# A four-network GNN kernel on one Trainium2 core: the third mask row loaded ahead of the bias, the second attention unit summed ahead of the third turn, and the count diagonal read behind the next rows

## What is computed

```python
def _gat_layer(x, src, dst, W, a_src, a_dst, bias, concat):
    h = (x @ W).reshape(N, H, C)
    al_s = jnp.einsum('nhc,hc->nh', h, a_src)
    al_d = jnp.einsum('nhc,hc->nh', h, a_dst)
    e = jax.nn.leaky_relu(al_s[src] + al_d[dst], NEG_SLOPE)
    m = jax.ops.segment_max(e, dst, num_segments=N)
    ex = jnp.exp(e - m[dst])
    denom = jax.ops.segment_sum(ex, dst, num_segments=N)
    alpha = ex / (denom[dst] + 1e-16)
    out = jax.ops.segment_sum(h[src] * alpha[:, :, None], dst, num_segments=N)
    ...
    return out + bias
loops = jnp.arange(N, dtype=edge_index.dtype)
src = jnp.concatenate([edge_index[0], loops])
dst = jnp.concatenate([edge_index[1], loops])
h = jax.nn.elu(_gat_layer(x, src, dst, W1, att_src1, att_dst1, b1, concat=True))
out = _gat_layer(h, src, dst, W2, att_src2, att_dst2, b2, concat=False)
```

## Time and profile before

| | |
|---|---|
| median of 3 runs | 3439.72 us (3429.32 to 3456.67) |
| profiled execution, its own time | 3440.88 us |
| its span in the trace | 3439.1 us |
| PE, DVE, ACT, POOL busy | 3217.4, 2175.2, 1337.0, 931.8 us |
| mean granted clock of PE | 0.961 |

### The profile page before, as it was taken

The page is one execution under the profiler, slowest core; times in us unless marked ns, Lnnn a source line. Parts: engine busy times, 40 slices in busy tenths (PEclk is TensorE's granted clock), DMA queues, the critical chain, the costliest instruction groups (busy, mean ns, idle before and its releaser), DMA issues. The chain is left out here.

```text
span 3439.1 us, 61776 instructions
## 1 busy us (share of the span) xinstructions
PE 3217.4 (94%) x20813; PEld 3007.6 (87%) x20813; DVE 2175.2 (63%) x4034; ACT 1337.0 (39%) x2527; POOL 931.8 (27%) x968
## 2 busy tenths in 40 slices
PE   6888999999998999999998999999999897899997
PEld 6876777888887999999997899999988586899997
DVE  7888546667686631018877610228878565499998
ACT  1344233333323121115546411124446330488885
POOL 1102633544545330005447400014447200000000
PEclk9988999999999999999999999999999889899998
DMA  3133344223222353347777643348767400300001
GB/s 81 46 90 121 113 128 106 64 66 108 59 50 69 90 153 100 102 131 236 238 215 234 178 132 103 103 152 244 242 193 237 140 30 15 74 1 0 0 0 46
DMA packets 164966, 386.06 MB, mean 112 GB/s; under 512 B 34418, under 2 KB 103583, under 8 KB 164758
## 3 DMA queue, kind: packets, MB, share of 16 engines
q0 software_dynamic: 47200, 173.39, 16.9%
q1 hardware_dynamic: 80074, 147.20, 15.2%
q10 hardware_dynamic: 37484, 62.75, 6.0%
HBM read 283.93 MB, written 99.32 MB: 111 GB/s over the span
## 5 line engine op out<-in xcount | busy, mean ns | idle before, releaser
L1872 PE MATMUL bank<-w_hi,xT_hi 128*125 128x384 f32 x1920 | 650.6, 339 | 0.0
L1873 PE MATMUL bank<-w_lo,xT_hi 128*125 128x384 f32 x1920 | 648.9, 338 | 0.0
L1874 PE MATMUL bank<-w_hi,xT_lo 128*125 128x384 f32 x1920 | 648.9, 338 | 0.0
L1560 ACT COPY arena<-bank 125x384 f32<-125x384 f32 x320 | 153.8, 480 | 793.8 <-PE bank L1874 765.3
L830 POOL DMA_INDIRECT arena<-y_early,edges x204 | 229.7, 1126 | 817.7 <-DMA y_late<-arena 320.0
L904 DVE SCALAR_TENSOR_TENSOR row_lo<-arena,edges,row_hi 128x768 fp32r<-128x768 f32 x300 | 304.1, 1014 | 125.5 <-ACT row_hi L873 84.1
L2339 DVE CAST w_hi<-w_raw 128x2304 fp32r<-128x2304 f32 x35 | 47.6, 1359 | 517.3 <-PE bank L1874 511.0
L743 ACT ACTIVATE arena<-arena,low 125x1250 f32<-125x1250 f32 x170 | 227.7, 1339 | 334.1 <-DVE low L755 334.1
L1872 PEld LDWEIGHTS bank<-w_hi,xT_hi 128*125 128x125 f32 x1920 | 356.8, 186 | 0.0
L1873 PEld LDWEIGHTS bank<-w_lo,xT_hi 128*125 128x125 f32 x1920 | 356.6, 186 | 0.1
L1874 PEld LDWEIGHTS bank<-w_hi,xT_lo 128*125 128x125 f32 x1920 | 356.6, 186 | 0.1
(11 more groups left out here) (359 smaller groups left out, 6636.6 us busy)
## 6 DMA issues: line engine op xcount, KB each, us to landing
y_early<-arena SPq DMA_DIRECT2D x200, 180.0 KB
w_raw<-in_L_gnn_W_dram ACTq DMA_DIRECT2D x30, 1152.0 KB, 6.3
arena<-own_mask_d SPq DMA_DIRECT2D x50, 585.9 KB
y_late<-arena SPq DMA_DIRECT2D x120, 180.0 KB
h_d<-arena ACTq DMA_DIRECT2D x40, 250.0 KB
arena<-in_L_gnn_W_dram SPq DMA_DIRECT2D x5, 1536.0 KB, 10.5
arena<-h_d ACTq DMA_DIRECT2D x30, 250.0 KB
wadj_d<-arena SPq DMA_DIRECT2D x10, 625.0 KB
```

The lines of the kernel that those rows point to most:

```text
L1872: pe.matmul(b, xT_hi[:, k, v], w_hi[:, h, k], start=(k == 0), stop=False)
L1873: pe.matmul(b, xT_hi[:, k, v], w_lo[:, h, k], start=False, stop=False)
L1874: ins = pe.matmul(b, xT_lo[:, k, v], w_hi[:, h, k], start=False, stop=(k == KD - 1))
```

## The change

Four edits. SP issues the load of mask row 2 ahead of the wait for `al_done` and the bias load. PE sums unit 1 ahead of turning unit 2 and the hidden row of unit 0; ACT runs the exponential of unit 2 behind the high parts of unit 1 instead of ahead of them. DVE reads the count diagonal behind the hot rows of window 4d + 3 instead of ahead of them. No instruction is added or removed.

```diff
--- before.py
+++ after.py
@@ -1096,11 +1096,12 @@
                     load_mask(0)
             sp.wait_ge(h_made, unit(H0 * NT - 1))
             load_mask(1)
-            sp.wait_ge(al_done, H0 * NT)
-            load_b1(0)
             for u in range(2, H0 * NT):
                 h, d = divmod(u, NT)
                 load_mask(u)
+                if u == 2:
+                    sp.wait_ge(al_done, H0 * NT)
+                    load_b1(0)
                 if h and d == 2:
                     sp.wait_ge(hidden_ready, unit(h * NT - 1))
                     load_b1(h)
@@ -1482,9 +1483,11 @@
                         act_hidden_high(act, u - 2)
                     if more:
                         load_next(h + 1, s)
+                    if u == 1:
+                        act_unit_exp(act, u + 1, u + 1, score[:, (u + 1) % 2])
                     if s == 1:
                         act_elu(act, u - 1)
-                    if s + 2 < NT:
+                    if s + 2 < NT and u:
                         act_unit_exp(act, u + 2, u + 2, score[:, u % 2])
                     if more and s == 2:
                         act_row_turn(act, h + 1, bank[2][0:NT, 256:256 + P])
@@ -1811,6 +1814,8 @@
                     u = h * NT + s
                     if more and s == 3:
                         pe.wait_ge(al_ready, h + 2)
+                    if u == 2:
+                        pe_sum(pe, u - 1, [3 + (u - 1) % 2], lambda t: [h_hi[t]], lambda t: [h_lo[h % 2][t]])
                     if s < NT and (s or not h) and u != 1:
                         pe_unit_turn(pe, u, score[:, s % 2])
                     if s >= 2:
@@ -1818,7 +1823,7 @@
                     if more and s == NT:
                         pe.wait_ge(turned_taken, piece(u - 1, 2))
                         pe_s_row(pe, h + 1, 0)
-                    if 1 <= s <= NT:
+                    if 1 <= s <= NT and u != 2:
                         pe.wait_ge(hidden_ready, unit(u - 3))
                         if u == 1:
                             pe.wait_ge(s_row_ready, 1)
@@ -2133,7 +2138,6 @@
                 if d >= 1 and i == 3:
                     if d >= 3:
                         finish_own(d - 3)
-                    count_own(d - 1)
                 if d >= 2 and i == 1:
                     take_log(d - 2)
                 at = d * P + WIN * i
@@ -2146,6 +2150,8 @@
                                                  feat[:, bass.ds(t, 1), R:FC].rearrange("p o c -> p (o c)").unsqueeze(2).to_broadcast([128, 4, WIN]),
                                                  op0=ALU.is_equal, op1=ALU.mult)
                         dve.tensor_scalar(hot_src[:, k], iota_half, edge[:, SRC, bass.ds(t, 1)], None, op0=ALU.is_equal).then_inc(hot_ready[k], 1)
+                if d >= 1 and i == 3:
+                    count_own(d - 1)
                 if w:
                     weight_sum(w - 1)
             weight_sum(NW - 1)
```

## The result

| | before | after |
|---|---|---|
| median of 20 runs | 3437.89 us (3426.75 to 3458.37) | 3419.02 us (3408.87 to 3448.40) |
| ratio of after to before | | 0.9944, 95% interval 0.9924 to 0.9965 |
| profiled execution, span | 3440.88 us, 3439.1 us | 3441.28 us, 3439.5 us |

The change makes the kernel 18.9 us faster; 3421 had been forecast. But the profiled execution of the changed kernel is among the slowest four of its twenty, and as long as that of before. So a comparison of the two spans would say "no change", and the traces have to be compared stage by stage.

What follows compares the result with a forecast made beforehand. PE sets the pace in projection and attention; DVE and PE wait for each other in counting. Counting 14 + attention 6.6 - clock 2 = 18.6, say 19 us: 3440 - 19 = 3421, range 3404 to 3437 (8 in 10).

Steps and rivals of the forecast that it cites:

- rival 2: Counting gets its clock back: 14 + 9 = 23 us there and attention 6.6, giving 3410; chance 0.12.
- Counting, idle time: Counting, read behind hot rows: PE's late hot rows mostly vanish, 14 us won (low end 8, high end 17.7).
- what ACT takes back: Third block of counting: ACT's count copy, straight behind the logarithms, takes back about 0.6 of PE's 1.3 us.
- Counting, clock: Counting: behind one wait PE ran at 1.2 GHz, 0.54 us more a tile, 2.2 a window; not in the sum.
- Recurring waits: By the skill's rule on waits recurring at each step, counting wins more than 14 us and attention only 2.3.
- Mask row 2: Start of attention: load issued near 498.2 instead of 508.48, landing near 506.5, in time for DVE at 511.45.
- The new order: First attention units, played through with old durations: hidden turn of unit 1 at 535.1 against 541.71, gain 6.6 us.
- The uncovered wait: Ahead of L612, the logit row's turn: PE stands 4.4 us for DVE's low parts of unit 2.
- The clock behind that wait: Product part 0 in attention may run at the lower clock, up to 4.3 us more; 2 charged.
- Slower: Counting: PE stands a little in every window and drops to half clock more often, 3452; chance 0.04.
- waits that only move: Counting: DVE's waits only move from L2100 to its ring slots, 3435; chance 0.03.

Runs made afterwards that it cites:

- the second group: Runs on another chip, with the changed kernel unedited against the kernel before: medians 3418.65 against 3452.67 us, ratio 0.9910 (0.9875 to 0.9944).
- the second pair: Second profiled executions of the unedited kernel before and the unedited changed kernel: projection starts at 310.8 and 294.6 us.
- three waits: Kernel before with DVE's wait for ACT's copy also at the heads of the second and third windows: 3511.84 us, ratio 1.0214.
- order only: Kernel before with only the new order on PE and ACT, mask row 2 still loaded late: ratio 1.0008 (0.9972 to 1.0044).
- logits last: Changed kernel with the last network's four-column logit products behind all wide feature products: median 5.6 us above the changed kernel's.
- before again: Kernel before, unedited, profiled a second time: median 4.2 us above the kernel before in the same group, projection at 310.8 us.

## Why the prediction was right, point by point

- **The total.** 3421 forecast, 3419.0 measured, range 3404 to 3437. The ratio says 12 to 26 us faster; the second group puts the change at 34, the interval there 19 to 43. A sum of 19 was at the low side of what all groups together show. That 3421 was met within 2 us is partly luck: the stages of the traces add up to 23 or 24 us (16.2 or 17.3 in counting, 6.9 in attention), inside both intervals but not 19, and rival 2, with 0.12, describes counting better than the forecast does.
- **Counting, idle time.** 14 us had been taken from PE's sum in the earlier trace rows; PE's waits for hot rows fell by 12.2, to 4.3 where about 2 had been expected, and the nine waits of DVE are gone. But other waits, for ACT's count copies above all, came in their place, and PE's idle time fell by 8.4 us only (9.0 in the second pair). The term was too high by 5 to 6 us: of what ACT takes back 0.6 had been seen, in one block, and not charged. The read ended where it was expected to: ACT waits in the first two blocks alone, 0.56 and 1.85 us, where up to 1.6 had been expected once or twice.
- **Counting, clock.** Here the sum had nothing and was too low. Projection starts 17.3 us earlier in the first pair of executions and 16.2 in the second, where 14 had been forecast. What the idle time doesn't explain is the clock, 8.9 and 7.2 us: rival 2's mechanism, which I had given 0.12, and nearly its size of 9. The experiments show it from both sides, with more waits (36.8 us of idle time cost 72.9) and with the idle time filled. I had the row for it, 1.33 against 0.79 us a tile, and treated it as a case apart rather than as a term of the sum.
- **Recurring waits.** The Trainium skill ("TensorE: Matmul & The Clock Gate", section "HAM oscillation") describes waits that recur at each step and throw PE back to the slow clock; they are waits for DMAs of several us. By it, as the prediction read it, counting was to win more than 14, and it won 16.2 and 17.3; that waits of 1.3 to 2.2 us do the same is shown by the traces here, not by that section. Attention was to win only 2.3 by it and won 6.9: PE did slow down behind its new wait, but for 1.6 us.
- **Mask row 2.** Issued with mask row 1 right at unit 0's mask step, no wait ahead of unit 2's: as forecast. That it now shares the queues with mask row 1 did no harm: it was there when DVE wanted it.
- **The new order.** Behind the projection's last product the steps were forecast at 20.9 (sum of unit 1), 27.9 (turn 2), 34.3 (L612) and 40.7 us (hidden turn); they came at 20.8, 27.9, 33.4 and 40.4. The uncovered wait is 3.81 us, forecast 4.4. The hidden turn was to come 21 us earlier and came 26.7 earlier; beyond its 14 and 6.6 these are 3.3 in counting, 2.5 in the projection and 0.3 here.
- **The clock behind that wait.** Charged at 2 us; the 24 products took 5.8 us instead of 4.25 (522.39 to 526.64 for the next 24), so 1.6. But I also charged it on top of ACT's row turn, which I had let hold PE until 39.4 us. ACT was through at 37.9, and PE's slow products filled just that time. So attention gave 6.9, not 6.6 - 2 = 4.6.
- **Slower, or waits that only move.** Neither came. PE's clock in counting rose, and DVE's waits for its ring slots (L2149 behind L1734) are 1.8 us in four, where they were 2.5 in seven.
- **Not foreseen:** the feature stage, which in one execution takes back 33 us and in another nothing. It is in neither the sum nor the range, and can move a single execution by more than the change is worth.

## What to carry to other kernels

Price a recurring short wait of the matmul engine at its idle time plus the slower products that follow it, when the granted clock in the rows behind it says so; here the second part was as large as the first (8.9 and 8.4 us in the change, 36.2 and 36.8 with three waits). Read both parts over the same work, as busy and idle time up to a common point: the sum of one kind of wait (12.2 us) overstated the idle time won. Move a late load before reordering the work around it: the load alone gave 5.5 of 6.9 us, the order alone nothing. Compare traces stage by stage before trusting two spans, since one stage at the other clock level (33 us) can hide the whole change (19 us).

## What the runs showed of the hardware

- PE, busy all the time, ran the feature products in 72.3 us at granted clock 0.53, and the same instructions in 38.9 us at 1.00 in another execution. In order only it was busy 20.00 of 20.00 us with counting's products at 0.50. The Trainium skill ("TensorE: Matmul & The Clock Gate", section "What's actually happening") has 2.4 GHz for a busy engine; these stretches, and the narrow products alone at 0.50, don't agree with it, as far as busy is what the profile calls busy.
- The 60 products of 4 columns, 120 matmuls in the trace, took 22.3 us, nearly all at half clock (2930.7 to 2952.9 in logits last), or 0.19 us a matmul: with a weight load of its own, a narrow product is far from free.
- Filling a wait of 1.3 us with 12 useless turns did not lengthen the kernel, and the granted clock of the stage went from 0.91 (before again) to 0.95.
